# Four layers of a graph network: tiles in their natural order around a circle, one gather for each chunk of edges in passes one to three, and slots handed on by SyncE

## The reference

```
Z = h @ W;                      agg[d] = sum of Z[s] * weight over edges (s, d);   x += relu(agg)         # pass 1
h' = h @ W.T + b;               agg[d] = sum of dis[s]*dis[d]*h'[s] over edges and loops;  x += relu(agg) # pass 2
agg[d] = sum of h[s];           x += relu((h + agg) @ W1 + b1) @ W2 + b2                                  # pass 3
8 heads: softmax over the edges of a node of leaky_relu(scores), weighted sum of (h @ Ws + Wb)[s];  x += ..  # pass 4
```

## Time and profile before

| | us |
|---|---|
| median of 3 runs | 2604.97 (2604.46 to 2607.5) |
| the profiled execution's own time | 2599.57 |
| its span, first to last instruction | 2598.2 |
| pass 1, first to last gather | 114.9 to 678.6 |
| pass 2, first to last gather | 704.2 to 1263.5 |
| pass 3, first to last gather | 1279.4 to 1832.6 |
| busy over the span: PE, DVE, POOL | 2247.8 (87%), 1596.4 (61%), 1809.6 (70%) |

### The profile page before, as it was taken

How to read it: one execution, slowest core, us unless ns; L and a number is a source line. 1 busy time by engine, 2 the same in 40 slices (tenths; PEclk the granted TensorE clock), 3 DMA queues, 4 the chain that set the end, 5 groups by cost and what they waited for, 6 DMA issues and landing times.

```text
span 2598.2 us, 32288 instructions
## 1 busy us (share of the span) xinstructions
PE 2247.8 (87%) x8238; PEld 1144.0 (44%) x8238; DVE 1596.4 (61%) x3866; ACT 330.8 (13%) x497; POOL 1809.6 (70%) x1878
## 2 busy tenths in 40 slices
PE   6889999989688878888579999998889899998887
PEld 5635444434322222222135555555488744443333
DVE  7687766665335444333235554555688688887777
ACT  4400000000000000000000000000188300000000
POOL 0277777777477777777577777777376677777776
PEclk9999999999899999999879999999999799999999
DMA  6497777787577787777677777777465678887776
GB/s 171 138 298 206 209 208 206 207 273 224 156 217 211 243 234 214 234 221 220 186 214 225 233 235 234 231 232 232 129 172 153 190 222 239 238 267 221 222 220 192
DMA packets 212758, 557.09 MB, mean 214 GB/s; under 512 B 55432, under 2 KB 56833, under 8 KB 212600
## 3 DMA queue, kind: packets, MB, share of 16 engines
q0 software_dynamic: 144448, 462.60, 61.2%
q1 hardware_dynamic: 66970, 90.10, 11.2%
q10 hardware_dynamic: 1182, 2.33, 0.3%
HBM read 515.28 MB, written 39.59 MB: 214 GB/s over the span
## 4 chain that ended last, share of the span: by engine, by line
PE 55%; DMA 20%; POOL 9%; DVE 8%; issue 7%; ACT 1%; SPq 0%; ACTq 0%; DVEq 0%; POOLq 0%
PE tiles L1514 30%; DMA ring<-table,src_t 19%; POOL ring L1848 7%; PE upper L1476 5%; PE last_bank L1657 3%; PE tiles L1510 3%; PE last_bank L1476 2%; PE tiles L1511 2%; POOL ring L1915 2%; PE upper L1747 2%; PE upper L1465 1%; DVE ring L1285 1%; PE upper L1686 1%; DVE x L1259 1%; PE tiles L1747 1%
## 5 line engine op out<-in xcount | busy, mean ns | idle before, releaser
L1848 POOL DMA_INDIRECT ring<-table,src_t x1320 | 1274.1, 965 | 470.2 <-issue 266.6
L1514 PE MATMUL tiles<-ring,sel 128*125 128x512 f32 x2562 | 1317.0, 636 | 190.7 <-DMA ring<-table,src_t 99.9
L1514 PEld LDWEIGHTS tiles<-ring,sel 128*125 128x125 f32 x2562 | 415.9, 191 | 811.2 <-issue 804.0
L1915 POOL DMA_INDIRECT ring<-table,src_t x401 | 387.2, 966 | 122.2 <-issue 81.4
L516 DVE TENSOR_TENSOR sel<-iota_bank,dl_t 128x500 f32<-128x500 f32 (+1 forms) x330 | 221.8, 674 | 395.7 <-PE tiles L1514 274.6
L1285 DVE TENSOR_TENSOR ring<-ring,iota_bank 128x512 f32<-128x512 f32 x388 | 254.4, 682 | 79.3 <-DMA ring<-table,src_t 77.3
L1510 PE MATMUL tiles<-ring,sel 128*125 128x512 f16 x440 | 178.5, 406 | 77.4 <-DMA ring<-table,src_t 66.6
L1511 PE MATMUL tiles<-ring,sel 128*125 128x512 f16 x440 | 172.1, 391 | 0.0
L1882 POOL DMA_INDIRECT big<-score_table,src_t x104 | 102.0, 981 | 74.7 <-issue 38.3
L808 DVE TENSOR_SCALAR sel<-node_iota,dl_t,w_t 128x125 f32<-128x125 f32 x440 | 135.8, 355 | 7.4 <-PE tiles L1514 7.1
L1510 PEld LDWEIGHTS tiles<-ring,sel 128*125 128x125 f16 x440 | 60.9, 139 | 160.5 <-issue 144.8
(11 more groups left out here) (362 smaller groups left out, 2641.2 us busy)
## 6 DMA issues: line engine op xcount, KB each, us to landing
ring<-table,src_t POOLq DMA_INDIRECT x1721, 3.8
table<-stage SPq DMA_DIRECT2D x50, 224.0 KB
table<-acc SPq DMA_DIRECT2D x50, 224.0 KB
acc<-dst_places SPq DMA_DIRECT2D x28, 256.0 KB
x<-dst_places SPq DMA_DIRECT2D x27, 256.0 KB
x<-in_x SPq DMA_DIRECT2D x25, 224.0 KB
kept_x<-x SPq DMA_DIRECT2D x25, 224.0 KB
x<-kept_x SPq DMA_DIRECT2D x25, 224.0 KB
```

What stands on the lines that cost most here:

```text
L1514: last = P.matmul(to, sel[:, n % SELS, :], rows, start=False, stop=True, skip_group_check=True)
L1848: G.indirect_dma_start(out=(ring16 if layer == 2 else ring)[:, n % RING, :], out_offset=None, in_=table[layer][:, :], in_offset=bass.Indir ...
L1915: G.indirect_dma_start(out=rows_at(i), out_offset=None, in_=table[3][:, :], in_offset=bass.IndirectOffsetOnAxis(ap=src_t[:, i:i + 1], axis ...
```

## The change

The tiles are no longer sorted: they run in natural order around a circle, from the tile where the steps are furthest ahead of an even share (`ahead`, `most`, `turn_at`). With the inputs as drawn every tile ends 0 or 1 steps before `ENDS[k]` (0 to 6 before the change). Neighbouring tiles now follow each other, and so the chunk at their boundary is gathered once and used by two consecutive steps: `GN` = 417 gathers in each of passes 1 to 3 (416 chunks, and the one at which the circle starts a second time), for the same 440 steps.

The slots of the ring are now those of gathers, 16 instead of 11 (`spare` has become part of `ring`). Neither PE nor POOL knows at build time which gather a step uses. So SP stands between them: for each gather it waits for the DMA (`pass_on`) and raises `landed`; and it waits for the last step of the gather two before (`give_back`, the step number from `last_row`, read into registers 20 at a time) and raises `freed`, on which POOL waits. PE's `step` takes tile and gather from one packed word, waits for `landed` up to that number, and takes the slot from the word's low four bits. SP's other work (x again, tile stores, weight loads) stands between the gathers, at numbers worked out from `ENDS`.

Beside that: DVE makes the new tables; POOL gathers four more groups of edge rows at the start; PE turns eight more small blocks and DVE copies two more tables (`turn_pairs`, `pair_tables`); ACT instead of SP issues the three `src_digits` stores; the `w3` loads move into pass 3; `fresh` becomes one semaphore for each pass. Pass 4 keeps its gathers, and its steps read the packed word.

```diff
-            def gather(layer):
-                for i in range(STEPS):
-                    n = STEPS * layer + i
-                    if n >= RING:
-                        G.wait_ge(stepped, step_value(n - RING))
+                for j in range(GN):
+                    if j >= SLOTS or layer and j == 0:
+                        G.wait_ge(freed, GN * layer + max(0, j - SLOTS + 1))
                     G.indirect_dma_start(
-                        out=(...)[:, n % RING, :], ... src_t[:, i:i + 1] ...).then_inc(got[n % RING], 16)
+                        out=(...)[:, slot_of(j), :], ... src_c[:, j:j + 1] ...).then_inc(got[slot_of(j)], 16)
...
             def step(layer, i):
-                t = step_tile(i)
+                word = step_word(i)
+                t = step_tile(word)
                 if layer < 3:
-                    P.wait_ge(got[r], got_value(n))
+                    P.wait_ge(landed[layer], word & (PACK - 1))
...
+                    rows = ring[:, bass.ds(word & (SLOTS - 1), 1), :] if layer < 3 else rows_at(i)
...
+            def pass_on(layer, j):
+                S.wait_ge(got[slot_of(j)], got_value(layer, j))
+                S.sem_inc(landed[layer], 1)
+
+            def give_back(layer, j):
+                if j % LOADED_TILES == 0:
+                    S.reg_load(last_regs, last_row[0:1, j:j + LOADED_TILES])
+                end = S.snap(last_regs[j % LOADED_TILES])
+                S.wait_ge(stepped, end + SIGNALS * layer)
+                S.sem_inc(freed, 1)
...
+            for j in range(GN):
+                pass_on(2, j)
+                if j >= 2:
+                    give_back(2, j - 2)
+                if j in W3_AT:
+                    ...
+                k = stores_at.get(j)
+                if k is not None:
+                    store_scores(k)
```

More of the change, by code:

```diff
@@ L98, in build, with reach @@
     ended = {end: k for k, end in enumerate(ENDS)}
+    scaled_at = []
+    for i in range(STEPS + 24):
+        if i > DEG_END and i % 2 == 0 and len(scaled_at) < sum(end <= i - 22 for end in ENDS):
+            scaled_at.append(i)
+    def reach(p):
+        return p - sum(end <= p for end in ENDS) + 1
     FW = RB * CE
@@ L196, in build @@
         bank += [upper[:, n, :] for n in range(NAGG)] + [last_bank[:, :]]
+        spare = ring[:, RING:SLOTS + 1, :]
         flat_ring = ring[:, :, :].rearrange("p a b -> p (a b)")
+        src_c = spare[:, 5, 0:GN].bitcast(I32)
+        last_row = den[0:1, :, :].rearrange("p t w -> p (t w)")[:, 0:STEPS].bitcast(I32)
+        chunk_rows = [spare[0:RS, b, 0:3 * CE].bitcast(I32) for b in range(RB)]
         dstf = b2_bc[0:RS, :].rearrange("p (b e) -> p b e", b=RB)
@@ L642, in step_tables @@
                     own.mark(V.tensor_copy(dstf[:, b, :], ri[:, CE:2 * CE]))
+                for b in range(RB):
+                    own.mark(V.tensor_copy(chunk_src[:, b, :], chunk_rows[b][:, 0:CE]))
                 V.wait_ge(v_own, own.n)
@@ L1557, in degree_group, with turn_pairs @@
                 last.then_inc(deg_sum, 1)
+            def turn_pairs():
+                for b in range(RB):
+                    last = P.transpose(bank[2][0:1, b * RS:(b + 1) * RS], last_step[:, b:b + 1], ident[0:RS, 0:RS])
+                last.then_inc(rows_turned, 1)
+                for b in range(RB):
+                    last = P.transpose(bank[3][:, b * RS:(b + 1) * RS], rsf[:, b, 0, :], ident[0:RS, 0:RS])
+                last.then_inc(rows_turned, 1)
             def open_banks():
@@ L1941, in store_tile @@
                 S.dma_start(low, rows_ap[TOP:TN]).then_inc(table_st[n % 3], 16)
+            last_regs = [S.alloc_register(f"last{n}") for n in range(LOADED_TILES)]
+            def pass_on(layer, j):
[4 more added lines that the diff above has]
+                    S.reg_load(last_regs, last_row[0:1, j:j + LOADED_TILES])
+                end = nc.s_assert_within(S.snap(last_regs[j % LOADED_TILES]), 1, STEPS,
+                                         skip_runtime_bounds_check_because="a chunk's last step is one of STEPS")
+                S.wait_ge(stepped, end + SIGNALS * layer)
+                S.sem_inc(freed, 1)
             S.wait_ge(pads, 3)
@@ L1996, in sync_program @@
             S.dma_start(ab_bc[:, :], ab_in.rearrange("(a h) -> a h", a=1).to_broadcast([TN, H])).then_inc(w_in_sb, 16)
-            for k in range(TILES):
-                if k == G1_AT:
+            stores_at = {reach(ENDS[k] + 24): k for k in range(TILES)}
+            stored_till = sum(at < GN for at in stores_at)
+            for j in range(GN):
+                pass_on(1, j)
+                if j >= 2:
+                    give_back(1, j - 2)
+                if j == G1_AT:
                     S.wait_ge(flags, 1)
@@ L2007, in sync_program @@
                         S.dma_start(raw_wh[:, b, :, :], Ws_in[:, b * 128:(b + 1) * 128, :].rearrange("h p j -> p h j")).then_inc(ws_in, 16)
-                if k == G2_AT:
+                if j == G2_AT:
                     S.wait_ge(wa_ok, 1)
                     S.dma_start(raw_w, G2_in.rearrange("(k p) d -> p k d", p=128)).then_inc(b_in_sb, 16)
+                k = stores_at.get(j)
+                if k is not None:
+                    S.wait_ge(rows16, k + 1)
+                    store_tile(2 * TILES + k, z16(2 * TILES + k))
+            for j in range(GN - 2, GN):
+                give_back(1, j)
+            for k in range(stored_till, TILES):
                 S.wait_ge(rows16, k + 1)
```

244 lines of the change are left out of this document (170 added, 74 removed).

## The result

The changed kernel takes 2611.66 us (median of 20 runs, 2603.78 to 2618.45), the kernel before beside it 2606.34 (20 runs). The ratio is 1.0017, with a 95% interval of 1.0009 to 1.0025 (the two medians alone give 1.0020): the change makes the kernel slower by 0.2%, which is little, but more than the noise. 2540 was forecast. The 23 gathers a pass were saved as forecast. Passes 1 and 2 gave some 54 us, the start took 10, and pass 3 with its tail took 53.

What follows compares the result with a forecast made beforehand. POOL's gather issuing was taken to bound all three passes. Gains of 23.5, 28.7 and 15, less 1 and 1.5 added, make -64.7 us: profiled 2599.6 becomes 2534.9, and the median, 5.4 above, 2540 (2526 to 2554, chance 0.50).

Steps and rivals of the forecast that it cites:

- POOL's issuing bounds the kernel, 23 gathers a pass are saved: Passes 1 to 3: POOL issues a gather every 1.257 to 1.281 us; 23 fewer a pass save 87.6 us together.
- POOL as the bound everywhere: Rival 1, all passes: PE catches up in pass 3 and POOL stays the bound; 2520 us, chance 0.22.
- Pass 1: First pass: 29.5 us saved, less 3 for x again and 3 for PE trailing at the end; gain 23.5.
- x again: Pass 1: SP issues one tile's two x loads with each of the first 25 gathers; +3 us (0 to +15).
- Pass 2: Second pass: PE has 6.1 us of slack a tile, 16 slots cover the weight loads; gain 28.7, gathers last 530 us.
- Start: Before the first gather: extra edge-row gathers, DVE instructions, turns and table copies mostly hide; +1 us (0 to +4).
- Unit prices of the hand-over: SP: 0.25 us a gather, 1.5 per load of 20 registers, 2.5 for five issues; round from PE's step to `landed` 0.55.
- Pass 3: Third pass: PE has 1.5 us a tile to spare, hand-over wants 2.05; 14 us lost, gain 15 (0 to 29).
- The tail: Behind pass 3: the 36 us tail grows by about ten, or POOL shows gaps that SP releases.
- Register loads as a cause: Pass 3: SP's register load, 0.83 times a tile, starves PE by about 0.4 us a tile.
- rival 2: Passes 1 and 3: SP holds PE longer than its issues take; pass 3 gains nothing, pass 1 half; 2567 us, chance 0.20.
- Rival 3: Passes 1 to 3: SP's round becomes the pace, above 1.34 us a gather; at 1.40, 2681 us; chance 0.07.

Runs made afterwards that it cites:

- hand of eight: Changed kernel with the slot back; in pass 3 SP waits for gather j-8 instead of j-2 before passing on j+1: 2516.9 us, ratio 0.9687; again 2515.1, 0.9681.
- ACT's issues: Changed kernel with the slot back; in pass 3 ACT instead of SP issues the five stores of each of the first 20 tiles: 2531.2 us, ratio 0.9726.
- spread issues: Changed kernel with the slot back; in pass 3 SP's five store issues of a tile spread over five gathers: 2544.0 us, ratio 0.9787.
- loads of five: Changed kernel with the slot back; SP reads registers five at a time, not 20: 2607.3 us, ratio 1.0017; together with ACT's issues 2528.5 us, 0.9713.
- the slot back: Changed kernel with count and number of the tiles made in two slots of DVE's first phase again, not one: 2596.1 us, ratio 0.9989.
- four in hand: Changed kernel with the slot back; in pass 3 SP waits for the end of gather j-4 instead of j-2: 2520.5 us, ratio 0.9690.
- a variant of the changed kernel: Changed kernel with the slot back and a hand of eight in all three passes: 3139 us on that chip, ratios 1.0150 and 1.0148; elsewhere 2520.4 us, 0.9703.

## Why the prediction was wrong, point by point

- *POOL's issuing bounds the kernel, 23 gathers a pass are saved*: right in passes 1 and 2, and in pass 3 as soon as PE is fed. The forecast for POOL as the bound everywhere was 2520; the hand of eight gives 2515 to 2517, beside 2599 to 2600.
- *Pass 1*: forecast -23.5, measured -28.7. The 3 us for x again and the 3 us of lag did not appear; the DMA engines moved 299 GB/s in the 48 us of the earlier trace rows. That passes 1 and 2 together come near the forecast, 54.2 for 52.2, is in part luck, since this miss and the next cancel.
- *Pass 2*: forecast -28.7 and 530, measured -25.5 and 533.8. A gather's issuing got dearer, 406.96 / 417 = 0.976 us against 425.40 / 440 = 0.967: 3.8 us in all. DVE's work is the same with fewer gathers beside it, which the prediction had said, and valued at 1.3 for all passes. That fits the rule of the Trainium skill cited there (SBUF — State Buffer, § SBUF: two separate sides), but no run took DVE's share apart.
- *Start*: forecast +1 (0 to +4), measured +9.9. The instructions were priced one by one and placed "beside PE-bound products". Missed: two merged slots move a wait of DVE one tile forward in its order.
- *Unit prices of the hand-over*: right. A give-back with a pass-on costs 0.23 us (1525.09 to 1525.32 in the chain; forecast 0.25); a register load 1.36 at the median and 2.25 at most (1.5); five issues 2.4 (2.5). The Trainium skill (Advanced Engine Details and Errata, § Network/Comms) has 50 to 100 ns for reading a semaphore; here the instruction with SP's wait and increment takes 17 ns (the line of L2055 above). Whether that is the act which the page prices, no run shows.
- *Pass 3*: this is the step that failed: "about 1.0 us of starving with the round", and from that, with the smaller terms, "2.05, 0.55 more than there is" and "25 x 0.55 = 14 us". The runs show 68.7 us over POOL's pace in its place, 2.75 a tile.
  - The stall itself was under-sized: 1.34 to 1.45 in the tile shown, and two, 1.36 and 1.88, where a register load follows the issues (before 1523.06 and 1525.59). Over the pass the gaps cost 42.8 us more than with a hand of eight, 1.7 a tile.
  - The price of a stall is more than the stall. Half clock, behind many of them, was in no term; PE's work takes 23.5 us longer with it, 0.94 a tile.
  - In the prediction's own balance, PE's work of 482.7 / 25 = 19.3 a tile was right (19.5). To it come 87.1 / 25 = 3.5 of idle time and 0.9 of slower matmuls, 4.4 where 2.05 was forecast.
  - The tile shown has its own split: 19.3 + 1.34 of stall + 1.7 of half clock + 1.05 for three steps 0.78, 0.83 and 0.73 long in the place of 0.43 (two directly behind the stall, one ten us later) = 23.4, and its period is 23.6. The last of these terms is not a general price: over the pass all but 2.4 us is explained without it.
  - That the stores' hold starts all this is shown by the runs with ACT's issues, spread issues and larger hands. The half clock goes with the stalls in fourteen runs, but no run took the clock apart from them.
- *The tail*: "grows by about ten, or POOL shows gaps": both came, 13 us, and 106.8 us of gaps released by SP. So did PE's idle time "once a tile, about 1 us, beside SP's five issues", only longer.
- *Register loads as a cause* (0.4 us a tile): loads of five left pass 3 at 598.5, and beside ACT's stores they gave 525.6 for 527.5; no cost that the runs show.
- *Rivals*: rival 2 named the place (SP holds PE longer), but gave as reasons a late result of DVE or a longer round. In the tile shown the five issues run without a wait for 2.4 us, as forecast, and PE starts 0.53 us behind the first pass-on (1428.68 to 1429.21), where 0.55 was forecast for the whole round. It priced pass 3 at no gain, and expected pass 1 to suffer, which it did not. Rival 3 (SP's round as the pace) did not come: with a hand of eight the same SP keeps up with 1.26 us a gather. The chances were 0.01 for a change within 5 us and 0.07 for slower; the medians are 5.3 us apart.
- *Where the choice was made*: the prediction saw that PE has two gathers in hand and five issues take longer, and treated the number as given by the kernel. It is the parameter on which the change turns: with the slot back, two gives 0.9989 of the kernel before and four gives 0.9690.

## What to carry to other kernels

When an engine starts to hand resources from one to another, compare its longest single hold, not its mean load, with what the receiver has in hand, and give the receiver a hand that covers the hold: here 2.4 us against two f16 steps, and four gathers cured it. Price a stall of PE as the stall, plus the lower clock that may follow it: here, over the pass, 1.7 us a tile of gaps came with 0.9 of slower matmuls. When code in an engine's fixed order is merged, look at which waits move forward with it.

## What the runs showed of the hardware

- A stall of 1.45 us of PE was followed by 3.4 us of half clock, beginning 1.1 us after its end, while PE was busy again. Over pass 3, 30 to 34 gaps of 1 us and more came with 95 to 124 us of half clock, 11 to 21 gaps with 33 to 52. The Trainium skill (TensorE: Matmul & The Clock Gate, § Part 1: The HAM clock gate) says that the lower level is the default and activity releases it. The trace agrees as far as the two levels go, 1.00 and 0.50 in the windows above, and the fall behind a stall fits it. With four in hand a stall of 1.33 was not followed by such a stretch in the window of 1475 to 1500 (clock 1.00), so a stall of this length does not always bring it.
- A load of 20 registers takes SP 1.19 to 2.25 us while gathers run (the line of L2060).
- One chip ran the kernel before 19% slower and a variant of the changed kernel 25% slower, with single register instructions of PE's sequencer at up to 1.4 us (median 36 ns, as elsewhere).
